# A decoder layer with routed experts: second expert weights fetched per tile instead of kept on chip

## The reference, cut to what matters

```python
def _moe_mlp(x, gate_w, gate_b, w1, w2):          # w1 (8, 256, 1024), w2 (8, 1024, 256)
    xf = x.reshape(b * n, d)
    logits = xf @ gate_w + gate_b
    one_hot = jax.nn.one_hot(jnp.argmax(logits, axis=-1), E, dtype=xf.dtype)
    h = jax.nn.gelu(jnp.einsum('td,edh->teh', xf, w1), approximate=True)
    y = jnp.einsum('teh,ehd->ted', h, w2)
    out = jnp.einsum('te,ted->td', one_hot, y)
    return out.reshape(b, n, d)
...
x = x + _moe_mlp(_layernorm(x, ln2_w, ln2_b), gate_w, gate_b, w1, w2)
```

## Time and profile before

| | us |
|---|---|
| median of 3 runs | 1683.42 (1682.92 to 1687.5) |
| the profiled execution | 1689.58 |
| its span in the profile | 1687.7 |
| gate, from its first issue to the first instruction of route | 1273.8 to 1346.4 |
| route, to the first instruction of experts | 1346.4 to 1370.7 |
| experts, to the last scatter's issue | 1370.7 to 1683.7 |

### The profile page before, as it was taken

The page is one execution under the profiler, slowest core; times in us unless marked ns, Lnnn a source line. Parts: engine busy times, 40 slices in busy tenths (PEclk is TensorE's granted clock), DMA queues, the critical chain, the costliest instruction groups (busy, mean ns, idle before and its releaser), DMA issues. The chain is left out here.

```text
span 1687.7 us, 45723 instructions
## 1 busy us (share of the span) xinstructions
PE 1554.3 (92%) x18260; PEld 1087.5 (64%) x18261; DVE 1141.6 (68%) x1749; ACT 850.1 (50%) x1505; POOL 380.5 (23%) x662
## 2 busy tenths in 40 slices
PE   6999699997886999999999999999998849999997
PEld 3554356654544366666666666666666739889886
DVE  2547379998662988889888889888865643232322
ACT  1221144432443488888888888888884302222211
POOL 3110211110342111111111111111110115555553
PEclk9999599998998799999999999999999869999999
DMA  6000200000133111111111111111104845556562
GB/s 205 1 0 0 66 1 1 0 1 1 76 130 109 36 38 41 40 39 36 38 40 41 37 39 38 39 41 41 35 18 141 270 145 173 195 181 194 181 198 66
DMA packets 82399, 125.53 MB, mean 74 GB/s; under 512 B 24339, under 2 KB 48533, under 8 KB 82230
## 3 DMA queue, kind: packets, MB, share of 16 engines
q1 hardware_dynamic: 76614, 107.77, 21.2%
q0 software_dynamic: 5616, 15.34, 2.7%
HBM read 96.56 MB, written 26.08 MB: 73 GB/s over the span
## 5 line engine op out<-in xcount | busy, mean ns | idle before, releaser
L1255 DVE TENSOR_REDUCE sb_m_mx<-banks 128x1 f32<-128x1024 f32 x512 | 603.4, 1220 | 70.7 <-PE banks L1123 62.9
L1221 ACT ACTIVATE sb_m_pT<-banks 128x512 f32<-128x512 f32 x1024 | 556.6, 595 | 117.9 <-PE banks L1150 106.8
L1150 PE MATMUL banks<-sb_m_q,sb_m_k 99*32 99x512 bf16 x4096 | 467.2, 381 | 1.0 <-ACT sb_m_pT L1221 0.5
L1123 PE MATMUL banks<-sb_m_k,sb_m_q 96*32 96x512 bf16 x4096 | 367.9, 388 | 12.8 <-DMA sb_m_k<-k_parts 10.4
L1165 PE MATMUL banks<-sb_m_pT,sb_m_v 128*32 128x256 f32 x4096 | 314.3, 378 | 0.7 <-ACT sb_m_pT L1221 0.7
L1150 PEld LDWEIGHTS banks<-sb_m_q,sb_m_k 99*32 99x32 bf16 x4096 | 178.7, 96 | 79.8 <-ACT sb_m_pT L1221 6.0
L1123 PEld LDWEIGHTS banks<-sb_m_k,sb_m_q 96*32 96x32 bf16 x4096 | 160.2, 96 | 93.0 <-DVE sb_m_mx L1255 17.5
L1165 PEld LDWEIGHTS banks<-sb_m_pT,sb_m_v 128*32 128x32 f32 x4096 | 177.2, 109 | 58.3 <-ACT sb_m_pT L1221 1.2
L1787 ACT ACTIVATE sb_e_hT<-banks 128x512 f32<-128x512 f32 x78 | 46.6, 597 | 238.7 <-PE banks L1746 235.1
L1757 PE MATMUL banks<-w,sb_e_hT 128*128 x624 | 144.2, 384 | 8.2 <-ACT sb_e_hT L1787 3.9
L1093 POOL CAST sb_m_mx_parts<-sb_m_mxT 8x128 bf16<-8x128 f32 x64 | 18.1, 283 | 591.4 <-issue 563.5
(11 more groups left out here) (215 smaller groups left out, 1878.0 us busy)
## 6 DMA issues: line engine op xcount, KB each, us to landing
w<-in_w SPq DMA_DIRECT2D x47, 1024.0 KB, 9.2
sb_m_q<-q_parts SPq DMA_DIRECT2D x384, 32.0 KB, 1.8
sb_m_k<-k_parts SPq DMA_DIRECT2D x384, 32.0 KB, 1.8
q_parts<-sb_c_parts SPq DMA_DIRECT2D x24, 256.0 KB, 2.2
k_parts<-sb_c_parts SPq DMA_DIRECT2D x24, 256.0 KB, 2.2
X<-in_x SPq DMA_DIRECT2D x4, 1024.0 KB, 10.6
x_rows<-X SPq DMA_DIRECT2D x8, 512.0 KB, 9.9
z_rows<-sb_g_zs SPq DMA_DIRECT2D x8, 512.0 KB, 5.5
```

What stands on the lines that cost most here:

```text
L1123: mm = pe.matmul(ps[2 * (k % 2) + h][c:c + 32, :], q_s[0:R, i, k * P + c:k * P + c + 32], k_s[0:R, i, h * 512:(h + 1) * 512], start=True, ...
L1150: mm = pe.matmul(ps[rotating(use)][c:c + 32, :], k_s[:, i2, m * P + c:m * P + c + 32], q_s[:, i2, h * 512:(h + 1) * 512], start=True, stop ...
L1221: act.activation(pT[:, m, h * 512:(h + 1) * 512], ps[rotating(f"b{m}{h}")][:, :], ACT.Exp).then_inc(exped, 1)
L1255: dve.tensor_reduce(mx[:, par % 2, k:k + 1], pz[:, 2 * (k % 2):2 * (k % 2) + 2, :].rearrange("p q n -> p (q n)"), AX.X, ALU.max).then_inc( ...
```

## The change

The tensor `w2` for all eight experts and its loads in `gate` go. In their place stands `w2` with three buffers of 1 MB and a semaphore each. `route` fetches w2 for tiles 0 to 2, each behind its w1. In `experts` SP fetches w1(j+1) when up(j-2) is through, then w2(j) when down(j-3) is through, and so on in turn. `down` waits for its buffer and addresses it by q; TensorE reads no number any more.

```diff
@@ gate, SP
                 sp.dma_start(z_rows, zs[:, g % 2, :, :]).then_inc(z_stored[g % 2], 16)
-                sp.dma_start(t["w2"][:, g, :, :], dram["w2"][g].rearrange("(k p) n -> p k n", p=P)).then_inc(t["w2_in"], 16)
@@ route, SP
                 sp.dma_start(w1[:, j, :, :], dram["w1"][ds(e, 1), :, :].rearrange("o (k p) n -> p (o k) n", p=P)).then_inc(w1_in[j], 16)
+                sp.dma_start(w2[:, j, :, :], dram["w2"][ds(e, 1), :, :].rearrange("o (k p) n -> p (o k) n", p=P)).then_inc(w2_in[j], 16)
@@ experts, SP
-            def load(j, q):
+            def load(name, dst, signal, j, freed, value):
                 e = sp.value_load(owner[0:1, ds(j, 1)], min_val=0, max_val=E - 1)
-                sp.wait_ge(h_done, 2 * (j - W + 1))
-                sp.dma_start(w1[:, q, :, :], dram["w1"][ds(e, 1), :, :].rearrange("o (k p) n -> p (o k) n", p=P)).then_inc(w1_in[q], 16)
-
-            with sp.Fori(1, J // W) as it:
+                sp.wait_ge(freed, value)
+                sp.dma_start(dst, dram[name][ds(e, 1), :, :].rearrange("o (k p) n -> p (o k) n", p=P)).then_inc(signal, 16)
+
+            def load_up(j, q):
+                load("w1", w1[:, q, :, :], w1_in[q], j, h_done, 2 * (j - W + 1))
+
+            def load_down(j, q):
+                load("w2", w2[:, q, :, :], w2_in[q], j, y_done, j - W + 1)
+
+            load_up(W, 0)
+            with sp.Fori(1, J // W - 1) as it:
                 for q in range(W):
-                    load(it * W + q, q)
+                    load_up(it * W + q + 1, (q + 1) % W)
+                    load_down(it * W + q, q)
+            for j in range(J - W, J):
+                if j + 1 < J:
+                    load_up(j + 1, (j + 1) % W)
+                load_down(j, j % W)
@@ experts, TensorE
-            def down(j, q):
-                e = pe.value_load(owner[0:1, ds(j, 1)], min_val=0, max_val=E - 1)
+            def down(j, it, q):
                 pe.wait_ge(summed, 1 + j)
+                pe.wait_ge(w2_in[q], 16 * (it + 1))
                 for m in range(HT):
                     if m % 4 == 0:
                         pe.wait_ge(h_copied, 2 * j + m // 4 + 1)
                     mm = pe.matmul(ps[6][:, 0:D], hT[:, q, m, :],
-                                   w2[:, ds(e, 1), m, :].rearrange("p o n -> p (o n)"), start=(m == 0), stop=(m == HT - 1))
+                                   w2[:, q, m, :], start=(m == 0), stop=(m == HT - 1))
                 mm.then_inc(y_done, 1)
...
-            pe.wait_ge(w2_in, 16 * E)
@@ decoder
-            tensors(attention, [("w2", [P, E, HT, D], F32), ("logits", [P, NT, E], F32), ("token_from", [P, J], U32),
+            tensors(attention, [("logits", [P, NT, E], F32), ("token_from", [P, J], U32),
...
-            tensors(attention, [("w1", [P, W, KT, HT * P], F32)])
+            tensors(attention, [("w1", [P, W, KT, HT * P], F32), ("w2", [P, W, HT, D], F32)])
             t["w1_in"] = [attention.enter_context(nc.semaphore(f"w1_in{i}")) for i in range(W)]
+            t["w2_in"] = [attention.enter_context(nc.semaphore(f"w2_in{i}")) for i in range(W)]
```

More of the change, by code:

```diff
@@ L1480, in route @@
         "before", "prefer", "starts", "count", "token", "slot"))
-    w1, w1_in, tables_in = t["w1"], t["w1_in"], t["tables_in"]
+    w1, w1_in, w2, w2_in, tables_in = t["w1"], t["w1_in"], t["w2"], t["w2_in"], t["tables_in"]
     TABLES = 16 * len(t["tables"])
@@ L1769, in _ @@
                     turn(j + 2, it + (q + 2) // W, (q + 2) % W)
-                    down(j, q)
+                    down(j, it, q)
             for q in range(W):
@@ L1776, in _ @@
                     turn(j + 2, J // W - 1, q + 2)
-                down(j, q)
+                down(j, J // W - 1, q)
         @block.scalar
@@ L1879, in decoder @@
                 run(self_attention)
-            tensors(attention, [("w2", [P, E, HT, D], F32), ("logits", [P, NT, E], F32), ("token_from", [P, J], U32),
+            tensors(attention, [("logits", [P, NT, E], F32), ("token_from", [P, J], U32),
                                 ("token_to", [P, J], U32), ("owner", [1, J], I32)])
-            t["w2_in"] = attention.enter_context(nc.semaphore("w2_in"))
             t["tables_in"] = attention.enter_context(nc.semaphore("tables_in"))
```

## The result

| | before | changed |
|---|---|---|
| median | 1684.26 (1682.92 to 1687.5, 4 runs) | 1732.49 (1727.41 to 1739.97, 4 runs) |
| ratio | | 1.0276, 95% interval 1.0249 to 1.0303 |
| profiled execution | 1689.58, span 1687.7 | 1739.97, span 1738.2 |

The changed kernel is 2.8% slower, where 1717 us (2.0%) was forecast. The profiled execution of the changed kernel is the slowest of its four, with a granted clock of 0.945 over the whole span against 0.950 to 0.952 in the others.

A forecast was written before the change was run, and what follows sets the result against it. Bound: a latency loop through z's gather, 7.70 us a tile. Terms +32 (tiles), +1.5 (start), -0.5 (end) sum to +33: 1723 us for the profiled execution, 1717 against the median; range 1668 to 1735.

The forecast's parts named there:

- The loop: Expert tiles: a two-tile latency loop through z's gather, 15.11 us with the read exposed, sets the pace, not TensorE's 7.25.
- The collision: Expert tiles: z's gather waits behind a whole w2 fetch every other tile, mean 8.65 us a tile, +32 us.
- Turns packet by packet: DMA queues in expert tiles: by the skill's rule gathers are hardly held up; main term -15, first rival's 1669 us, chance 0.24.
- the 34 tiles: Main term, down products 2 to 36: tiles of 8.65 instead of 7.70 us, +32 us, between +26 and +38.
- might lose its full clock: Part of the 1735 us rival: TensorE, idle 16% of the time, loses full clock; no chance of its own given.
- scatter and gather of x piling up: Part of the 1735 us rival: they queue behind w1 and w2, z behind them, 0.6 us on long tiles (+10).
- The gate: Eight w2 loads leave the gate: taken as zero, up to 2 us could be won if a store drains sooner.
- The start: Before the experts: six loads instead of three make the first gather of z land later, +1.5 us (0 to 2).
- The end: Last tiles: nothing is fetched and the last exposed read goes, -0.5 us.
- The gain of the read: Expert tiles: number read leaves TensorE, 7.70 to 7.25 us a tile, 15.3 us won if nothing else moved.

The follow-up runs named there:

- turning GpSimd's order: Kernel before, with GpSimd gathering z ahead of x in each step, expert number still read on TensorE: 1669.65 us, ratio 0.9903.
- moving the read alone: Kernel before, with tile j's expert number read on TensorE ahead of up product j+1 instead of down product j: 1677.89 us, ratio 0.9945.
- half the fetch: Changed kernel, each w2 fetch in the experts stage carrying only the first half of the rows (0.5 MB): 1695.98 us, ratio 1.0049.
- the fetches that nobody needs: Kernel before, with the changed kernel's w2 fetches added into three buffers that nobody reads: 1763.09 us, ratio 1.0440.
- long runs: Changed kernel, w2 fetched in the experts stage in runs of 8 KB per partition instead of eight of 1 KB: 1715.89 us, ratio 1.0168.
- the held fetch: Changed kernel, SP issuing the fetch of w2(j) only when the gathered rows z(j) have landed: 1735.27 us, ratio 1.0261.
- the fetch 1.5 us later: Changed kernel, each w2 fetch issued when the variance of the tile three before is done, not its down product: 1707.8 us, ratio 1.0114.
- the changed kernel with z first: Changed kernel, with GpSimd gathering z ahead of x in each step: 1685.52 us, ratio 0.9991.
- z first and long runs: Changed kernel, with z gathered ahead of x and w2 fetched in runs of 8 KB: 1681.73 us, ratio 0.9959.
- the run without fetches: Changed kernel, w2 not fetched again in the experts stage, tiles 3 to 38 using the three fetched before it: 1679.96 us, ratio 0.9949.

## Why the prediction was right, and what was mis-sized

*The loop.* Right. z's gather, not the read or TensorE, set 7.70 us: turning GpSimd's order gives 7.25 with the read in place, and moving the read alone gives 7.40.

*The collision.* Right in place and size. Every other gather of z stands behind a w2 fetch issued 0.2 to 0.5 us ahead of it and lands after 5.2 to 6.1 us; tiles were forecast at 9.7 to 10.4 and 7.25, and are 9.8 to 10.4 and 7.24, where the clock holds. The long ones take 10.04 us as mean, so without the clock a pair of tiles would come to 8.64 us each, where 8.65 was forecast. Traffic alone does it (ratio 1.044), and half the fetch takes more than half of the wait away (1.1 us left of 2.6).

*Turns packet by packet.* The queues show 498 packets of w2 in 1.4 us and none of the waiting gather. That is 31 for each of the sixteen engines, one behind the other, and each is a single run of 1 KB. The scatter and the gather of x, which stood behind w1, moved before most of w2 did. So the queues look as if they took turns, but by something near a whole transfer. The Trainium skill, DMA: Bandwidth & Descriptors, section Queues, rings and completion order, has each DMA engine take turns between its queues packet by packet, but its packet is a group of descriptors, typically about 9 to 17 and at most 64. The prediction read that packet as the profile's, a single run, and so made more of the contradiction than there is: if a descriptor is such a run, the trace shows more in a row than the page calls typical, and a whole w2 fetch, 64 runs for each engine, would just fit the page's limit. Whether the engines treat it as one packet no run here shows.

*The term that was too small* is the 34 tiles: +32 forecast, +46.3 measured. It was the clock, which stood among the rivals only ("might lose its full clock"). The other half of that rival, scatter and gather of x piling up for a further 0.6 us on long tiles, didn't come. So the point forecast was 15 us short, and the measured 1732 lies near the top of the range, 1735, which was put there for this rival. Stretch of one down product, clock in the third column from the end:

```profile
1541.80:1548.40 6.60, 4.22 (x36) 3.92 (x34) 1.60 (x5) 1.19 (x2) 3.55 (x6) 1.00 0.97 333
1548.40:1553.40 5.00, 5.00 (x17) 4.08 (x16) 0.73 (x2) 0.00 (x0) 1.57 (x3) 0.66 0.65 257
```

TensorE works 4.2 of 6.6 us at full clock and waits 2.4, and in the following five microseconds the granted clock is 0.66 of full speed, so for part of it at the lower level of 1.2 GHz; the down product takes 5.01 us instead of 3.32. Nine of the 17 short tiles are 8.6 to 8.9 us for this, 9 x 1.6 = 14 us, which is the difference. The other three executions, whose granted clock is higher, probably had fewer such pieces.

No run changed the clock alone, so that the waits bring it down is argued from the traces side by side. Behind the first turn, the traces of all runs have 33 down products ahead of the last one that are stretched to 4.6 to 5.0 us, and each stands right behind a wait for z of 1.97 to 3.22 us. None stands behind a shorter wait, but 31 waits of that length have none behind them. In the changed kernel, with waits of 2.5 to 3.1 us in every other tile, there are ten, the last of them outside the stretch; with the fetches that nobody needs 11; with long runs, whose waits are mostly 1.9 to 2.1, five; with the held fetch five. Half the fetch has no wait above 1.7 us and no such piece. Such a piece also came behind single waits: the fetch 1.5 us later, with nothing above 1.9 us until then, has one behind its only long wait, and the changed kernel with z first has one behind a wait of 2.36 us. In the run of the later fetch:

```profile
1676.31 0.24 PEld L1748 LDWEIGHTS banks<-ident_sb,sb_e_z 128*128 128x128 f32 x2 [2.78 <-DMA sb_e_z<-z_rows,sb_e_numbers]
1676.53 4.96 PEld L1769 LDWEIGHTS banks<-w,sb_e_hT 128*128 128x128 f32 x16
```

Yet one of 3.19 us in the run with z first and long runs has none. A prediction should price the clock where it makes TensorE wait like this again and again: here 14 us over 17 waits, 0.8 us for each as a mean.

*The other terms.* The gate: zero, as taken; its DMA share falls from 0.91 to 0.43 and route begins at 1346.1, where it began at 1346.4. The start: 1.5 was forecast, and the first turn is 1.6 us later, but only 0.8 of it reaches down product 0. The first long tile, +2.2, stands ahead of the 34 intervals and was in no term. The end: -0.5 forecast, +1.2 measured, again a down product at the lower clock. The gain of the read: in the run without fetches 9 us, not 15, since the loop at 7.19 us a tile leaves no room for gathers that land after 3.5 us.

## What to carry to other kernels

A stage may look bound by the engine that is 97% busy and yet be paced by a latency loop through a transfer; find it by walking back from one late instruction to the one of its own kind two tiles earlier, and add up the terms. Then a new transfer is dear above all by what it is issued just ahead of, and there by its whole length. The cheap cure is lead: put the gather that the next work waits for ahead of the one with slack, before adding or moving anything.

## What the runs showed of the hardware

- A gather issued 0.2 to 0.5 us behind a 1 MB fetch moved no packet until the fetch was nearly through, with runs of 1 KB as of 4 KB: landing 5.2 to 6.1 us instead of 2.8.
- w2 in runs of 8 KB instead of 1 KB shortened the long tiles by 0.6 us, from 10.0 to 9.4 as mean.
- In the traces of all runs 33 down products took 4.6 to 5.0 us instead of 3.32, the one looked at above at a granted clock of 0.66; each stood right behind a wait of 1.97 to 3.22 us, and 31 waits of that length had none behind them.
- The sixteen DMA engines carried 323 GB/s at 95% share over 262 us, and TensorE's tiles stayed at 7.2 us in three of four cases.
- In route SP's fetch issued fifth took 4.08 us to issue behind four others, where the one before it took 0.41:

```profile
1359.25 0.41 SPq L1525 DMA_DIRECT2D w<-in_w  x1
1360.42 4.08 SPq L1524 DMA_DIRECT2D w<-in_w  x1
```
